# Edge ranges searched partly inside the block loop, with their index on GpSimd and the loop unrolled

## Chip, cores, metric

One core of a Trainium2 chip runs the whole program. The metric is the time of one execution on the device in microseconds (us). Engines: TensorE (PE, its weight loads PEld), VectorE (DVE), ScalarE (ACT), GpSimd (POOL), SyncE (SP, which only issues DMAs here).

## What is computed

A graph layer and a mixture of experts over 6250 nodes of width 256, with 100000 edges of 96 features whose destinations `dst` are sorted:

```python
out1 = segment_sum(edge_attr, dst)            # per node
out2 = where(cnt > 0, segment_max(edge_attr, dst), 0)
out3 = out1 / maximum(cnt, 1)
h = concatenate([ln_x, out1, out2, out3, u[0]], axis=1)
x1 = x + relu(h @ W1 + b1) @ W2 + b2 + ln_x   # ln_x = layernorm(x)
y = layernorm(x1)                             # then top 2 of 16 experts
out = x1 + layernorm(y + moe(y)) * gamma + beta
```

The destinations are `6250 * u**2` of a uniform u, so low nodes have many edges and high nodes few.

## The kernel before

Three stages follow each other.

**Opening.** The 6250 nodes are 50 tiles of 125 (TILES), two to a block (25 blocks, MACROS), and the blocks are worked from the high nodes down. For every node the kernel must know at which edge its range starts. It is found in two steps. ScalarE compares each node with the heads of 625 rows of 160 edges (count_heads, line 815) and picks the row (pick_rows, 830 and 832). GpSimd fetches that row of `dst` for the 125 nodes of a tile by an indirect DMA (line 614), and ScalarE counts in it (count_row, line 824). This goes in ten groups of 5 tiles; SR holds ten fetched rows. GpSimd issues all 50 fetches before it goes on (lines 607 to 615); ScalarE counts all 50 before its first moments (line 878). VectorE turns the counts into start edge, row numbers IX of the two scans, chunk number gatei, and the factors cp, has and rch (index, lines 1420 to 1447): for 20 tiles behind its first chunk of edges, for the other 30 behind its second. SyncE moves each node's start to the node before it (nextn, lines 465 and 466).

**Block loop.** Two chains run side by side. VectorE scans the edges in ten chunks of 128 pieces of 80 edges, also from the end: running sums (line 1381), running maxima (line 1385) and the carry over the pieces (1396 to 1406). SyncE stores sums, maxima and carries to DRAM and then counts up chunk_done (line 470). For each block i GpSimd gathers, by six indirect DMAs (lines 631 to 633), the rows of both scans and the carry at IX. Before that it reads the block's chunk number, copies the block's index columns (line 623), waits for so many chunks and takes one of ten branches. Its order in a block is rows_step: add_rows(i-1) (660), residual(i) (677, 679), cut(i+1) (638), norm1(i+1) (651 to 655), join(i+1) (642 to 646), norm2(i-1) (665 to 670), gather(i+2). The blocks run in pairs inside a hardware loop, hence the copied columns.

ScalarE's order is gnn_step: moments of the next block (878, 883), carry_in(i+1) (861; 865, whose input is the cut; 867; 869), the first four relus of block i (913), moments2 (922, 927), mask_rows(i+1) (893 to 899), the second four relus (913), and the copies of transposed tiles. TensorE does layer 1 in two halves of four banks (1160 to 1164), with the router (1193) between them, the transposes of the next block (1141, 1144), then layer 2 (1174). The second half of layer 1 reuses a bank that the first half's first relu frees.

**Experts.** 113 slots of 128 rows go through their expert's two matrices (1284, 1292), and a last norm follows.

SyncE, ScalarE and GpSimd each run strictly in the order written, so a wait holds up everything behind it on that engine.

## Time and profile before

| | us |
|---|---|
| median of 3 runs | 1287.15 (1284.53 to 1287.29) |
| the profiled execution | 1287.32, its span 1285.6 |
| TensorE busy | 1105.2 (86%) |
| VectorE busy | 803.1 (62%) |
| ScalarE busy | 647.5 (50%) |
| GpSimd busy | 802.0 (62%) |
| mean granted TensorE clock | 0.978 |

A profile comes from one execution. Times in it count from the start of the span. The chain of waits that the page prints gives half of the span to TensorE and a third to VectorE's scans. A wait in it is put down to the event seen last; where a semaphore had long been up, the line names it all the same, so waits are better read from the timeline of the waiting engine.

### The profile page before, as it was taken

To read this page: it belongs to the slowest core of one execution; us is meant where nothing else is said; L and a number is where in the kernel's file an instruction comes from. 1 tells how busy PE (TensorE), PEld (TensorE's weight loads), DVE (VectorE), ACT (ScalarE), POOL (GpSimd) and SP (SyncE) were. 2 spreads that over 40 slices of the span, in tenths; PEclk is the share of its full clock that TensorE was granted. 3 is DMA by queue.
4 is the path that set the end of the run, shared out by engine and by line. 5 is a ranking of instruction groups with operands and counts; after the bars stand their busy time and mean duration, and the time that the engine had idled before them with its cause. 6 is when DMAs were issued, how large, how long until landed. Compare 5 with 4: busy or idle time off the path is not lost.

```text
span 1285.6 us, 27773 instructions
## 1 busy us (share of the span) xinstructions
PE 1105.2 (86%) x6560; PEld 965.7 (75%) x6561; DVE 803.1 (62%) x3060; ACT 647.5 (50%) x1974; POOL 802.0 (62%) x1053
## 2 busy tenths in 40 slices
PE   2002999999999998999999999999999999999914
PEld 1001788888878887887888888889999999989801
DVE  4999999799889989970362401474322222247777
ACT  5863565666566655665665433222232323346544
POOL 4886657766755675666766425555666666656576
PEclk9999999999999998999999999999999999999966
DMA  9995668768767776479111046865666666689744
GB/s 318 279 300 191 238 232 313 254 258 294 257 256 255 285 249 223 173 263 306 46 45 40 28 134 220 303 242 173 203 214 212 204 215 207 217 279 298 249 171 153
DMA packets 131327, 282.71 MB, mean 220 GB/s; under 512 B 25900, under 2 KB 38576, under 8 KB 131114
## 3 DMA queue, kind: packets, MB, share of 16 engines
q1 hardware_dynamic: 94230, 218.41, 49.3%
q0 software_dynamic: 26048, 43.47, 11.1%
q10 hardware_dynamic: 10964, 19.96, 4.5%
q14 instruction: 63, 0.52, 0.1%
q8 instruction: 22, 0.36, 0.1%
HBM read 167.27 MB, written 114.25 MB: 219 GB/s over the span
## 4 chain that ended last, share of the span: by engine, by line
PE 50%; DVE 34%; DMA 6%; issue 5%; POOL 2%; ACT 2%; SPq 1%; POOLq 0%; DVEq 0%; ACTq 0%
PE ps L1284 14%; PE ps L1292 14%; DVE mem L1381 13%; DVE mem L1385 13%; PE ps L1174 5%; PE ps L1160 5%; PE ps L1162 5%; PE ps L1270 2%; DMA mem<-x_normed,mem 2%; DVE mem L1401 2%; PE ps L1210 1%; DMA mem<-piece_carry,mem 1%; DVE mem L1406 1%; DVE mem L1396 1%; DMA mem<-in_edge_attr_dram 1%
## 5 line engine op out<-in xcount | busy, mean ns | idle before, releaser
L1013 ACT ACTIVATE mem<-ps,mem 128x128 f32<-128x128 f32 x452 | 129.3, 368 | 285.1 <-PE ps L1284 283.2
L1284 PEld LDWEIGHTS ps<-mem 128*128 128x128 f32 x1808 | 217.8, 192 | 11.8 <-issue 5.9
L1284 PE MATMUL ps<-mem 128*128 128x128 f32 x1808 | 221.2, 276 | 4.1 <-issue 3.8
L1160 PE MATMUL ps<-mem 128*128 128x250 f32 x800 | 208.4, 383 | 16.4 <-ACT mem L913 14.9
L1292 PE MATMUL ps<-mem 128*128 x904 | 215.2, 381 | 3.7 <-issue 3.2
L1381 DVE TENSOR_TENSOR_SCAN mem<-ps,mem 128x80 f32<-128x80 f32 x960 | 208.0, 304 | 0.3
L1385 DVE TENSOR_TENSOR_SCAN mem<-ps,mem 128x80 f32<-128x80 f32 x960 | 207.8, 313 | 0.0
L1162 PE MATMUL ps<-mem 128*128 128x250 f32 x800 | 204.1, 378 | 0.0
L1174 PE MATMUL ps<-mem 128*125 128x256 f32 x800 | 181.0, 379 | 0.7 <-ACT mem L913 0.7
L1292 PEld LDWEIGHTS ps<-mem 128*128 128x128 f32 x904 | 162.9, 190 | 24.6 <-issue 6.9
L1160 PEld LDWEIGHTS ps<-mem 128*128 128x128 f32 x800 | 152.7, 194 | 35.8 <-ACT mem L913 16.8
L1162 PEld LDWEIGHTS ps<-mem 128*128 128x128 f32 x800 | 153.6, 192 | 18.6
L1174 PEld LDWEIGHTS ps<-mem 128*125 128x125 f32 x800 | 146.3, 188 | 21.1 <-ACT mem L913 1.1
L724 POOL DMA_INDIRECT expert_rows<-mem x90 | 90.9, 1010 | 99.1 <-DVE mem L1659 87.6
L1659 DVE TENSOR_TENSOR mem<-ps,mem 128x256 f32<-128x256 f32 x113 | 48.0, 425 | 148.6 <-PE ps L1292 145.0
L1652 DVE COPY mem<-ps 128x256 f32<-128x256 f32 x113 | 47.8, 423 | 145.9 <-PE ps L1270 142.2
L718 POOL DMA_INDIRECT mem<-x_normed,mem x94 | 93.9, 999 | 30.2 <-issue 15.0
L913 ACT ACTIVATE mem<-ps,mem 128x250 f32<-128x250 f32 x200 | 77.1, 468 | 48.9 <-PE ps L1164 48.9
L1141 PE MATMUL ps<-mem 125*128 125x125 f32 x100 | 20.6, 288 | 91.2 <-ACT mem L899 91.2
L631 POOL DMA_INDIRECT mem<-run_max,mem x50 | 63.7, 1275 | 46.4 <-issue 43.2
L1141 PEld LDWEIGHTS ps<-mem 125*128 125x128 f32 x100 | 11.6, 144 | 98.3 <-issue 98.3
L614 POOL DMA_INDIRECT mem<-in_dst_dram,mem x50 | 62.1, 1242 | 29.5 <-ACT mem L832 14.6
(279 smaller groups left out, 1672.7 us busy)
## 6 DMA issues: line engine op xcount, KB each, us to landing
mem<-in_L_ffn_w_dram SPq DMA_DIRECT2D x129, 512.0 KB, 9.6
run_sum<-mem SPq DMA_DIRECT2D x80, 480.0 KB, 5.6
run_max<-mem SPq DMA_DIRECT2D x80, 480.0 KB, 5.5
mem<-in_edge_attr_dram SPq DMA_DIRECT2D x72, 480.0 KB, 8.1
mem<-expert_rows SPq DMA_DIRECT2D x26, 256.0 KB, 5.0
x_rows<-mem ACTq DMA_DIRECT2D x25, 256.0 KB, 3.0
x_normed<-mem ACTq DMA_DIRECT2D x25, 256.0 KB, 4.0
mem<-in_x_dram ACTq DMA_DIRECT2D x24, 256.0 KB, 4.8
```

Source lines behind the costliest of these rows:

```text
L631: pool.indirect_dma_start(out=GM[b][:, a, :], out_offset=None, in_=s_max[0:edges], in_offset=last).then_inc(gathered[b], 16)
L718: pool.indirect_dma_start(out=XG[b], out_offset=None, in_=x2_d[0:rows], in_offset=bass.IndirectOffsetOnAxis(slot_now[b], 0)).then_inc(xg_g ...
L724: pool.indirect_dma_start(out=ya_d, out_offset=bass.IndirectOffsetOnAxis(into_now[b], 0), in_=YO[b], in_offset=None).then_inc(yo_stored[b] ...
L913: act.activation(H[:, hc, :], bank(H_BANKS[q][hc - q * QUAD], 0, M), ACT.Relu, bias=cbias[:, hc:hc + 1]).then_inc(h_ready, 1)
L1013: ins = act.activation(hT[b][:, c, :], bank(2 + b, c * P, (c + 1) * P), ACT.Relu, bias=eb1c[:, bass.ds(e, 1), c])
L1160: pe.matmul(h, W1x[:, c, hc * P:(hc + 1) * P], XT[b][:, c, :], start=(c == 0), stop=False)
L1162: pe.matmul(h, W1a[:, s, hc * P:(hc + 1) * P], AT[b][:, s, :], start=False, stop=False)
L1174: ins = pe.matmul(bank(5, a * D, (a + 1) * D, NT), H[:, hc, a * NT:(a + 1) * NT], W2[:, hc, :], start=(hc == 0), stop=(hc == HC - 1))
L1284: ins = pe.matmul(bank(2 + b, f * P, (f + 1) * P), w1now[q][:, c, f * P:(f + 1) * P], XgT[b][:, c, :], start=(c == 0), stop=(c == DC - 1))
L1292: ins = pe.matmul(bank(6 + b, 0, D), hT[b][:, c, :], w(c * D, D), start=(c == 0), stop=(c == FC - 1))
L1381: ins = dve.tensor_tensor_scan(out=Sb[:, ::-1, f], data0=keep[b][:, ::-1], data1=Eb[b][:, ::-1, f], initial=0.0, op0=ALU.mult, op1=ALU.add)
L1385: ins = dve.tensor_tensor_scan(out=Eb[b][:, ::-1, f], data0=bound[b][:, ::-1], data1=Eb[b][:, ::-1, f], initial=-FMAX, op0=ALU.min, op1=AL ...
```

## The change

The tiles are split in three. The 20 first ones (FIRST_TILES) and ten more (LATER_TILES) are fetched and counted ahead of the loop, 30 fetches instead of 50; the 20 last (LAST_TILES) are fetched two per block in blocks 0 to 9, into four buffers of their own (SRL), by seek_late on GpSimd, and counted by ScalarE in the same block, ahead of the second relus (count_late). ScalarE's head counts all stay ahead of the loop; the row counts of the sixth five tiles stand behind head group 7 and ahead of head groups 8 and 9, and behind these come block 0's moments.

The index of the first 20 tiles runs on GpSimd, between its 25th and its 26th fetch, as 32 operations each waited for, with the two moves of start edges as DMAs of GpSimd. A power of -1 takes the place of the reciprocal there. The index of the next ten tiles stays on VectorE, behind its second chunk. That of the last 20 runs on GpSimd in four parts, between residual and cut of blocks 10, 11, 12 and 13.

GpSimd's block loop is written out for 25 blocks. Its gathers read the index columns in place. They wait for a number of chunks fixed per block (SCANNED); a branch on the chunk number falls back to all ten chunks if more than that were needed. For the inputs here the fixed number is as large as the needed one or up to three larger.

```diff
-    LATE = TILES - 4 * ST
+    FIRST_TILES, LATER_TILES = slice(TILES - 4 * ST, TILES), slice(TILES - 6 * ST, TILES - 4 * ST)
+    LAST_TILES = slice(0, TILES - 6 * ST)
+    SOUGHT = LAST_TILES.stop // 2
+    EARLY_GATHERS = 6
...
+    SCANNED = [1 if i < 4 else min(LEVELS, 1 + (24 * (i - 2) + 10) // 52) for i in range(MACROS)]
...
+        minus_one = k.take(4 * ST, parts=NT)
...
+        SRL = a.take(4, ROWE, parts=NT, dt=I32)
+        late_junk = [a.take(ROWE, parts=NT) for _ in range(2)]
...
+        def floors(e, op, out, v, n, shift_by):
+            op(e.tensor_scalar(out, v, 1.0 / n, (shift_by + 0.5) / n - 0.5, ALU.mult, ALU.add))
+            op(e.tensor_scalar(out, out, ROUND, None, ALU.add))
+            op(e.tensor_scalar(out, out, ROUND, None, ALU.subtract))
+        def start_edges(e, op, c):
+            op(e.tensor_scalar(startn[:, c], rowf[:, c], float(ROWE), 0.5 * ROWE, ALU.mult, ALU.add))
+            op(e.tensor_scalar(tA[:, c], rows_seen[:, c], 0.5, None, ALU.mult))
+            op(e.tensor_tensor(startn[:, c], startn[:, c], tA[:, c], ALU.add))
+        def start_rows(e, op, c):
+            op(e.tensor_copy(endn[:, c.start:c.stop:2], startn[:, c.start + 1:c.stop:2]))
+            op(e.tensor_scalar(tA[:, c], startn[:, c], float(E - 1), None, ALU.min))
+            floors(e, op, tB[:, c], tA[:, c], T, 0)
+            floors(e, op, tC[:, c], tB[:, c], P, PAD)
+            op(e.tensor_scalar(gatei[:, c.start // 2:c.stop // 2], tC[0:1, c.start:c.stop:2], -1.0, float(CHUNKS), ALU.mult, ALU.add))
+            op(e.tensor_scalar(tC[:, c], tC[:, c], -2.0 * P * T, None, ALU.mult))
+            op(e.tensor_tensor(tA[:, c], tA[:, c], tC[:, c], ALU.add))
+            op(e.tensor_scalar(IX[:, c, 0], tA[:, c], float(T * (PAD + FULL * P)), None, ALU.add))
+        def next_pieces(e, op, c):
+            op(e.tensor_scalar(tB[:, c], tB[:, c], 1.0, None, ALU.add))
+            op(e.tensor_scalar(cp[:, c], tB[:, c], float(T), None, ALU.mult))
+            op(e.tensor_scalar(tB[:, c], tB[:, c], float(PIECES - 1), None, ALU.min))
+            floors(e, op, tC[:, c], tB[:, c], P, PAD)
+            op(e.tensor_scalar(tC[:, c], tC[:, c], -2.0 * P, None, ALU.mult))
+            op(e.tensor_tensor(tB[:, c], tB[:, c], tC[:, c], ALU.add))
+            op(e.tensor_scalar(IX[:, c, 1], tB[:, c], float(PAD + FULL * P), None, ALU.add))
+        def edge_counts(e, op, c, one_over):
+            op(e.tensor_copy(endn[:, c.start + 1:c.stop:2], nextn[:, c.start:c.stop:2]))
+            op(e.tensor_tensor(cp[:, c], endn[:, c], cp[:, c], ALU.subtract))
+            op(e.tensor_scalar(cp[:, c], cp[:, c], 0.0, 1.0, ALU.max, ALU.min))
+            op(e.tensor_tensor(tA[:, c], endn[:, c], startn[:, c], ALU.subtract))
+            op(e.tensor_scalar(has[:, c], tA[:, c], 1.0, None, ALU.min))
+            op(e.tensor_scalar(tA[:, c], tA[:, c], 1.0, None, ALU.max))
+            one_over(tB[:, c], tA[:, c])
+            op(e.tensor_tensor(rch[:, c], tB[:, c], has[:, c], ALU.mult))
...
-                if isinstance(s, int) and s < 2:
-                    lo, hi = ((LATE, TILES), (0, LATE))[s]
-                    sp.wait_ge(starts_ready, s + 1)
-                    sp.dma_start(nextn[0:NT - 1, lo:hi], startn[1:NT, lo:hi]).then_inc(ends_got, 16)
-                    sp.dma_start(nextn[NT - 1:NT, lo:hi], startn[0:1, lo + 2:hi + 2]).then_inc(ends_got, 16)
+                if isinstance(s, int) and s == 1:
+                    c = LATER_TILES
+                    sp.wait_ge(starts_ready, 1)
+                    sp.dma_start(nextn[0:NT - 1, c], startn[1:NT, c]).then_inc(ends_got, 16)
+                    sp.dma_start(nextn[NT - 1:NT, c], startn[0:1, c.start + 2:c.stop + 2]).then_inc(ends_got, 16)
...
-            for n in range(GROUPS):
+            def seek(n):
...
-            pool.wait_ge(index_ready, 1)
-            def gather(i, g, b):
-                level = pool.value_load(gatei[0:1, bass.ds(MACROS - 1 - i, 1)], min_val=1, max_val=LEVELS)
-                hold(pool, turned, i + 1)
-                pool.tensor_copy(IXn[b], IX[:, bass.ds(2 * (MACROS - 1 - i), 2), :]).then_inc(ix_copied, 1)
-                pool.wait_ge(ix_copied, i + 1)
-                hold(pool, chunk_done, level * LEVEL)
-                for lv in range(1, LEVELS + 1):
-                    edges, pieces = lv * LEVEL * P * T, lv * LEVEL * P
-                    with pool.If(level == lv):
-                        for a in range(2):
-                            last, before = (bass.IndirectOffsetOnAxis(IXn[b][:, a, n:n + 1], 0) for n in range(2))
-                            pool.indirect_dma_start(out=GM[b][:, a, :], out_offset=None, in_=s_max[0:edges], in_offset=last).then_inc(gathered[b], 16)
-                            pool.indirect_dma_start(out=GS[b][:, a, :], out_offset=None, in_=s_sum[0:edges], in_offset=last).then_inc(gathered[b], 16)
-                            pool.indirect_dma_start(out=GC[b][:, a, :], out_offset=None, in_=carry[0:pieces], in_offset=before).then_inc(gathered[b], 16)
+            def seek_late(j):
+                if j == 0:
+                    pool.wait_ge(rows_ready, GROUPS)
+                if j >= 4:
+                    pool.wait_ge(late_counted, j - 3)
+                pool.indirect_dma_start(out=SRL[:, j % 4, :], out_offset=None, in_=dst2,
+                                        in_offset=bass.IndirectOffsetOnAxis(rowU[:, j:j + 1], 0)).then_inc(late_got[j % 4], 16)
+            ix = Steps(pool, index_step)
+            def op(ins):
+                ix.mark(ins)
+                ix.wait()
+            def pool_over(out, v):
+                op(pool.tensor_tensor(out, v, minus_one[:, 0:v.shape[1]], ALU.pow))
+            def end_edges(c):
+                pool.dma_start(nextn[0:NT - 1, c], startn[1:NT, c]).then_inc(pool_ends, 16)
+                pool.dma_start(nextn[NT - 1:NT, c], startn[0:1, c.start + 2:c.stop + 2]).then_inc(pool_ends, 16)
+            for n in range(5):
+                seek(n)
+            pool.wait_ge(row_counted, TILES - FIRST_TILES.start)
+            start_edges(pool, op, FIRST_TILES)
+            end_edges(FIRST_TILES)
+            start_rows(pool, op, FIRST_TILES)
+            next_pieces(pool, op, FIRST_TILES)
+            pool.wait_ge(pool_ends, 32)
+            edge_counts(pool, op, FIRST_TILES, pool_over)
+            pool.sem_inc(index_ready, 1)
+            seek(5)
+            def gather_rows(i, levels):
+                b, m = i % 2, MACROS - 1 - i
+                edges, pieces = levels * LEVEL * P * T, levels * LEVEL * P
+                pool.wait_ge(chunk_done, levels * LEVEL)
+                for a in range(2):
+                    last, before = (bass.IndirectOffsetOnAxis(IX[:, 2 * m + a, n:n + 1], 0) for n in range(2))
+                    pool.indirect_dma_start(out=GM[b][:, a, :], out_offset=None, in_=s_max[0:edges], in_offset=last).then_inc(gathered[b], 16)
+                    pool.indirect_dma_start(out=GS[b][:, a, :], out_offset=None, in_=s_sum[0:edges], in_offset=last).then_inc(gathered[b], 16)
+                    pool.indirect_dma_start(out=GC[b][:, a, :], out_offset=None, in_=carry[0:pieces], in_offset=before).then_inc(gathered[b], 16)
+            def gather(i):
+                m, near = MACROS - 1 - i, SCANNED[i]
+                if near == LEVELS:
+                    gather_rows(i, LEVELS)
+                else:
+                    level = pool.value_load(gatei[0:1, m:m + 1], min_val=1, max_val=LEVELS)
+                    with pool.If(level < near + 1):
+                        gather_rows(i, near)
+                    with pool.If(level > near):
+                        gather_rows(i, LEVELS)
...
-            def rows_step(i, g, b):
+            def rows_step(i):
+                g, b = i // 2, i % 2
                 more = not isinstance(i, int) or i + 1 < MACROS
                 norm = not isinstance(i, int) or i >= 1
                 if norm:
                     add_rows(i - 1)
                 residual(i, g, b)
+                if i < SOUGHT:
+                    seek_late(2 * i)
+                elif i == SOUGHT:
+                    pool.wait_ge(late_counted, 2 * SOUGHT)
+                    start_edges(pool, op, LAST_TILES)
+                    end_edges(LAST_TILES)
+                elif i == SOUGHT + 1:
+                    start_rows(pool, op, LAST_TILES)
+                elif i == SOUGHT + 2:
+                    next_pieces(pool, op, LAST_TILES)
+                elif i == SOUGHT + 3:
+                    pool.wait_ge(pool_ends, 64)
+                    edge_counts(pool, op, LAST_TILES, pool_over)
                 if more:
                     cut(*after(i, g, b))
                     norm1(i + 1)
                     join(*after(i, g, b))
+                if i < SOUGHT:
+                    seek_late(2 * i + 1)
                 if norm:
                     norm2(i - 1)
-                if not isinstance(i, int) or i + 2 < MACROS:
-                    gather(*after(i, g, b, 2))
+                if i + 2 < MACROS:
+                    if i + 2 == (TILES - FIRST_TILES.start) // 2:
+                        pool.wait_ge(index_ready, 2)
+                    gather(i + 2)
             pool.sem_inc(joined, 1)
-            gather(0, 0, 0)
+            gather(0)
             norm1(0)
             cut(0, 0, 0)
             join(0, 0, 0)
-            gather(1, 0, 1)
-            rows_step(0, 0, 0)
-            rows_step(1, 0, 1)
-            pool.wait_ge(index_ready, 2)
-            in_pairs(pool, MACROS, rows_step, ahead=3, first=2)
+            gather(1)
+            for i in range(MACROS):
+                rows_step(i)
...
+                if n - 2 < EARLY_GATHERS:
+                    count_row(n - 2)
+            def count_late(i, g, b):
+                for a in range(2):
+                    j = bass.ds(2 * i + a, 1)
+                    act.wait_ge(late_got[2 * b + a], (g + 1) * 16)
+                    if not isinstance(i, int) or i >= 1:
+                        act.wait_ge(late_counted, 2 * i + a - 1)
+                    act.activation(late_junk[a], SRL[:, 2 * b + a, :], ACT.Sign, bias=below[:, j], scale=-1.0,
+                                   accum_out=rows_seen[:, j]).then_inc(late_counted, 1)
...
+                if late:
+                    count_late(i, g, b)
...
+            gnn_step(0, 0, 0, late=True)
+            gnn_step(1, 0, 1, late=True)
+            in_pairs(act, SOUGHT, lambda i, g, b: gnn_step(i, g, b, EARLY_M - i, True), first=2)
+            in_pairs(act, EARLY_M, lambda i, g, b: gnn_step(i, g, b, EARLY_M - i), first=SOUGHT)
...
-            dve.wait_ge(row_counted, TILES - LATE)
-            op(dve.memset(startn[:, TILES:TILES + 2], float(E)))
-            index(LATE, TILES, 1)
             edges(1, 0, 1)
-            dve.wait_ge(row_counted, TILES)
-            index(0, LATE, 2)
+            dve.wait_ge(row_counted, TILES - LATER_TILES.start)
+            start_edges(dve, op, LATER_TILES)
+            dve.sem_inc(starts_ready, 1)
+            start_rows(dve, op, LATER_TILES)
+            next_pieces(dve, op, LATER_TILES)
+            dve.wait_ge(ends_got, 32)
+            edge_counts(dve, op, LATER_TILES, lambda out, v: op(dve.reciprocal(out, v)))
+            dve.sem_inc(index_ready, 1)
```

## Rows read from the trace of the kernel before

**Rows 1.** Windows: busy of PE, PEld, DVE, ACT, POOL; clock, DMA share, GB/s.

```profile
0.00:119.70 119.70, 9.29 (x27) 6.29 (x28) 100.09 (x437) 75.64 (x248) 78.90 (x89) 1.00 0.87 278
119.70:776.70 657.00, 638.84 (x3497) 546.15 (x3497) 482.03 (x2023) 383.65 (x1141) 406.47 (x510) 0.99 0.59 207
```

**Rows 2.** Timeline: start, length, engine, line, operation, [idle before <-releaser], us.

```profile
57.41 1.21 POOL L614 DMA_INDIRECT mem<-in_dst_dram,mem  x1 [0.30 <-issue]
...
97.48 1.22 POOL L631 DMA_INDIRECT mem<-run_max,mem  x1 [1.04 <-issue]
...
106.63 0.73 POOL L653 TENSOR_TENSOR mem<-mem 125x2 f32<-125x2 f32 x1
...
111.93 0.59 POOL L638 TENSOR_TENSOR mem<-mem 125x192 f32<-125x192 f32 x1 [4.29 <-DMA mem<-piece_carry,mem]
```

**Rows 3.** Timeline of ScalarE at the start.

```profile
71.65 0.76 ACT L815 ACTIVATE mem<-ps,mem 125x625 f32<-125x625 f32 x1
...
99.04 0.40 ACT L878 ACTIVATE mem<-mem 125x256 f32<-125x256 f32 x1
...
101.16 0.19 ACT L883 ACTIVATION_READ_ACCUMULATOR mem<-mem 125x1 f32 x1
```

**Rows 4.** Timeline of SyncE's queue: loads behind the first chunk.

```profile
78.36 4.02 SPq L434 DMA_DIRECT2D mem<-in_edge_attr_dram  x8
```

**Rows 5.** Landings from issue: L614; L631, then L633, over 95:200.

```profile
DMA to landing us min/median/max: 3.3/6.9/8.7
DMA to landing us min/median/max: 3.1/4.8/7.2
DMA to landing us min/median/max: 3.6/6.8/7.8
```

**Rows 6.** GpSimd's groups by line (count, busy us, mean ns); VectorE's timeline, index.

```profile
L653 POOL TENSOR_TENSOR mem<-mem 125x2 f32<-125x2 f32 x25 | 18.4, 735 | 2.1
...
L604 POOL TENSOR_SCALAR mem<-mem 125x50 f32<-125x50 f32 x1 | 0.4, 369 | 0.0
...
75.22 0.18 DVE L1417 TENSOR_SCALAR mem<-mem 125x20 f32<-125x20 f32 x1
```

**Rows 7.** Timeline of block 5: TensorE, ScalarE, GpSimd.

```profile
258.25 1.11 PE L1160 MATMUL ps<-mem 128*128 128x250 f32 x4
...
256.33 0.62 ACT L865 ACTIVATE mem<-mem 125x96 f32<-125x96 f32 x2
...
257.75 1.53 ACT L913 ACTIVATE mem<-ps,mem 128x250 f32<-128x250 f32 x4
...
266.05 1.55 ACT L913 ACTIVATE mem<-ps,mem 128x250 f32<-128x250 f32 x4 [0.79 <-PE ps L1164]
...
255.14 0.59 POOL L638 TENSOR_TENSOR mem<-mem 125x192 f32<-125x192 f32 x1
...
261.77 0.19 POOL L665 TENSOR_SCALAR mem<-mem 125x2 f32<-125x2 f32 x1 [1.47 <-ACT mem L927]
```

**Rows 8.** Waits (us, times, longest); TensorE's timeline; one window's clock.

```profile
PE ps L1160 <- ACT mem L913: 14.9, 13, 3.4
...
359.08 1.20 PE L1160 MATMUL ps<-mem 128*128 128x250 f32 x2 [2.00 <-ACT mem L913]
...
487.29 2.04 PE L1160 MATMUL ps<-mem 128*128 128x250 f32 x4 [3.39 <-ACT mem L913]
...
591.53 2.03 PE L1160 MATMUL ps<-mem 128*128 128x250 f32 x4 [2.79 <-ACT mem L913]
...
487.00:493.00 6.00, 5.71 (x16) 4.73 (x17) 6.00 (x30) 4.96 (x18) 3.33 (x7) 0.58 0.46 169
```

**Rows 9.** Timeline of GpSimd: first gather of block 6.

```profile
242.23 1.33 POOL L631 DMA_INDIRECT mem<-run_max,mem  x1 [1.38 <-issue]
```

**Rows 10.** Timeline of SyncE's queue: loads behind the third chunk.

```profile
200.44 4.18 SPq L434 DMA_DIRECT2D mem<-in_edge_attr_dram  x8
```

**Rows 11.** Timeline of VectorE: a turn of the scan loop begins.

```profile
249.70 0.25 DVE L1373 TENSOR_TENSOR ps<-mem 128x79 f32 x1 [5.76 <-issue]
```

48 lines of the change are left out of this document (7 added, 41 removed).

## Prediction

> **What bounds the kernel now.** I read the windows first. Up to 119.7 us TensorE does almost nothing (9.3 us busy), from 119.7 to 776.7 it is busy for 638.8 of 657 us [rows 1]. So the opening costs its full length, and in the block loop anything that makes TensorE wait costs its full length too. The expert stage behind it holds no step of the change and starts from what the loop delivers; I let it shift with the loop's end.
>
> Then the timeline of GpSimd at the start. The 26th of its 50 row gathers starts at 57.41 and each takes 1.21 us with 0.30 before it; block 0's own gathers start only at 97.48, behind all 50, and its cut runs at 111.93 [rows 2]. ScalarE ends block 0's moments at 101.35 (99.04 to 101.16 and 0.19), so it has about 10 us to spare there [rows 3]. The first chunk is known to be in DRAM at 78.36, when SyncE goes past its wait and loads the next edges [rows 4]. This is the room of the change: 78.4 against 97.5.
>
> Then one block of the loop, block 5, on three engines [rows 7]. TensorE begins its second half at 258.25 without a gap, and the relu that frees its bank started at 257.75. That relu stands in ScalarE's order behind the carries, whose sign step (line 865, 256.33) waits for GpSimd's cut (255.14 to 255.73). So the cut has 0.6 us of slack and the relu nearly none. Last the waits: TensorE stood at this place 13 times, 14.9 us in all; the large ones are 2.00, 3.39 and 2.79 us in blocks 9, 14 and 18, behind late carry gathers (block 0 has another of 2.5) [rows 8]. Of the other nine, 4.2 us together, the timeline puts 2.2 in blocks 1 to 9, 0.6 in blocks 10 to 13 and 1.4 behind.
>
> **Start: gathers.** GpSimd does 25 row gathers, done at 57.1. The 20 first counts are there by then. Now 32 small operations run on GpSimd, each waiting for itself: 3, then two DMAs, then 12, 9 and 8. The nearest rows are 0.73 us for the two-column power with 0.27 from the operation before it to its start [rows 2], and 0.37 for a plain operation with 50 columns [rows 6]; I take 0.29 a piece. The DMAs are not shown on GpSimd; between 0.35 and 1.5 us each, and I take 1.35, nearest to its own indirect ones. So 57.1 + 0.9 + 2.7 + 21 x 0.29 = 66.8, then 7 x 0.29 = 2.0 and the power with 20 columns. With two columns it takes 0.73, some 0.54 more than a plain operation [rows 6]. If that excess is per column, 20 take 5.6 us; if it is fixed, 0.7. I take 5.6, as the work is done element by element, and keep 0.7. Index ready at 75 (70). Five more row gathers: 83 (78). Gathers of block 0 start at about 84 (79), instead of 97.5.
>
> The Trainium skill, GPSIMD Engine Reference, section Performance versus the Vector engine, says that ordinary elementwise work is about twice as slow on GpSimd, with two software hops per instruction. Here 0.29 a piece stands against 0.21 from start to start on VectorE's index (0.18 long [rows 6]), less than the rule says. By the rule the 31 plain operations would take 13 us instead of 9, and the sum would be 4 us higher, 1295.
>
> **Start: ScalarE takes over.** It counts rows 25 to 29 only behind head group 7, and head groups 8 and 9 stand behind them. The last of these gathers starts at 81.4 (76.6) and lands 6.9 later [rows 5]; then come two head groups, each five counts of 0.76 and about 0.6 for picking the rows, 4.4, and 2.3 us of moments [rows 3]. That gives 99.9 (95.1) instead of 101.16. GpSimd's norm waits for them, and the cut stands behind it, 1.3 later: 101 (96) instead of 111.9. The gathered rows, starting 8 us after the first and landing 6.8 after that [rows 5], come at 98.5 and are no longer last. Gain 11 (16). VectorE's scan is about 8 us earlier because its first index is gone.
>
> **Blocks 1 to 9.** Two row gathers a block. The second stands in a gap of 1.47 us [rows 7] and is free. The first stands between residual and cut: 1.5 us less 0.6 of slack is 0.9, and I take 0.8, as the rows gathered for the next block leave GpSimd a little sooner. ScalarE's relu and with it TensorE's second half begin that much later, 1.8 in block 1, where TensorE waits already: 8 x 0.8 + 1.8 = 8. ScalarE's two counts of 0.41 stand ahead of the second relu, where it idles 0.79 [rows 7], if the second row has landed. It starts 3 us behind the first relu and must land in 5.2; the loop's first gathers took 3.1 to 7.2 [rows 5], over it by 0.4 on average: 3 in all. Against this, the gathers of a block leave earlier: the index copy, the hold and the chain of ten branches, 1.38 before line 631 in block 6 [rows 9] on top of what stands before line 623, shrink by 1.4 to 2.3 us, more in late blocks. The 2.00 and the 2.2 go, with 1.6 of low clock behind the first. Net: 11 less 5.8, 5 lost. Block 0 gains 0.6.
>
> **Blocks 10 to 13.** The index of the last 20 tiles stands between residual and cut: 3.6 us (3 operations, two DMAs), 3.5 (12), 2.6 (9), and 2.0 plus the power. Less 0.75 each that the block hides: 2.8, 2.7, 1.9 and 6.9 (2.0 with a fixed price), sum 14.3 (9.4). TensorE at rest also loses its clock: after the stop of 3.39 us the granted clock was 0.58 over 487 to 493, about half (1.2 GHz) for most of it [rows 8]; the stops of 2.8 and 2.0 cost 1.9 and 1.6 more in the same way, the one of 2.5 in block 0 nothing. I add 1.5 per block, 6. Less the old 0.6: 20 lost (15).
>
> **Blocks 14 to 24.** No added work, gathers 2 us earlier. Of 3.39 + 2.79 + 1.4 some 2 remain, and the low clock behind them (2.3 + 1.9) goes: 10 gained.
>
> **The new fixed chunk numbers.** Gathers now wait for a number of chunks fixed per block, up to three more than the block needs. Nearest is block 6 with chunk 3: its gathers start at 242.23, chunk 3 was there at 200.44 [rows 9, 10]. 42 us of distance, shrunk by 8 at most: nothing.
>
> **Sum**, in the profiled execution (1287.32 us, span 1285.6, practically the median 1287.15): -11 - 0.6 + 5 + 20 - 10 = +3.5, that is 1291 us. This case spans 1286 to 1298, with the clock price (0 to 8) and the DMAs on GpSimd (0.35 to 1.5 each).
>
> **Rivals.**
> 1. The power hardly grows with the columns. Start 16, blocks 10 to 13 15: -16 - 0.6 + 5 + 15 - 10 = -6.6, 1280.5. For it: the other GpSimd operations grow little (0.37 for 50 columns). Against: this one alone is 3.7 times as long at two. It decides at 3.9 us for 20 columns, where the sum is zero (each us of the power counts twice). Chance 0.26. This is the case on the other side.
> 2. The added work in the loop is hidden: the gap before line 660 and the earlier gathers take it up, and the cut isn't what the relu waits for. Then blocks 1 to 9 win 4 and blocks 10 to 13 cost 8: -11 - 0.6 - 4 + 8 - 10 = -17.6, 1270. Against: 0.6 us of slack is read directly. Chance 0.13.
> 3. ScalarE's loop becomes too long. In VectorE's loop there is a stop of 5.76 us without a releaser at every second turn [rows 11], which I read as code coming in. If ScalarE's body, longer by the counts, did this in its 4 turns of blocks 2 to 9, with 3 us of idle to take it up, that adds 4 x 2.8 = 11: 1302. ScalarE's rows show no such stop now. Chance 0.08. The Trainium skill, Runtime: NRT & Kernel Launch, section Instruction fetch mechanics, says that a taken branch to outside two pages of 256 instructions forces a fetch; by it this happens only if the body outgrows them, and GpSimd's unrolled order never pays it.
> 4. The row gathers land late throughout, as in the opening (6.9) instead of as in the loop: 9 x 1.7 instead of 3, 12 more: 1303. Chance 0.1.
> 5. The fixed chunk numbers do stop GpSimd after all: a block waits for a chunk, 10 us or more: 1300. Chance 0.03.
>
> **Chances.** Forecast 0.40; the rivals 0.26, 0.13, 0.08, 0.10, 0.03. The range from 1273 to 1302 leaves out part of rivals 2 and 4. A measurement can tell some 0.2% from no change, 2.6 us. Faster by more: rivals 1 and 2 but for their edge, 0.38. Within: 0.17, the lower end of the forecast and the upper end of rival 1. Slower by more: 0.45. Cases of both signs hold most of the chance, so the forecast's own range is 1286 to 1298.
>
> **What would show it.** Block 0's cut at 101 us, ScalarE idle before its count of row 25, index on GpSimd from 57 to 75 with one power near 5.6 us; about 0.8 us of wait at line 1160's second half in each of blocks 2 to 9, four waits of 2 to 7 us in blocks 10 to 13, fewer and shorter ones behind. Wrong, if the power takes under 2 us, if the cut in the blocks with row gathers ends before the sign step asks for it, or if the stage behind 776 us changes its own length.

## The result and the profile after

The changed kernel takes 1296.0 us (median of 6, 1293.3 to 1300.0) where the kernel before takes 1286.1 (median of 6, 1284.5 to 1288.7) on the same chip: ratio 1.0062, 95% interval 1.0033 to 1.0092. It is slower, by 0.6%, clear of noise. Its profiled execution took 1293.27 us, with a span of 1291.0; the span before was 1285.6, so the two traces differ by 5.4 us.

The windows of the changed kernel, to be read beside [rows 1] (busy of PE, PEld, DVE, ACT, POOL; granted clock, DMA share, GB/s):

```profile
0.00:108.00 108.00, 8.55 (x27) 5.99 (x28) 89.92 (x389) 64.96 (x204) 66.86 (x101) 0.57 0.89 293
108.00:770.00 662.00, 633.00 (x3439) 540.42 (x3440) 479.33 (x2044) 390.28 (x1176) 436.98 (x538) 0.98 0.59 204
770.00:1291.00 521.00, 468.50 (x3096) 421.50 (x3094) 221.91 (x603) 192.17 (x595) 319.68 (x460) 0.95 0.68 223
```

Before the loop TensorE has almost nothing to do up to 109.9 us instead of 119.8, and yet the span is longer, so what stands behind the opening must have lost more than the opening won. (The mean granted clock is 0.931 where the trace of before has 0.978. That difference lies in the opening, 0.57 against 1.00, where TensorE is busy for 9 us only; from the first transposes to the 25th block's it is 0.98 and 0.99.) To see where the time went, I took the start of every block's transposes (line 1255, line 1141 before) from TensorE's timeline and call the start of block n's "turn n". The stretch from turn 1 to turn 10 is then TensorE's work of blocks 1 to 9. Five of the turns, of the changed kernel:

```profile
109.92 0.65 PE L1255 MATMUL ps<-mem 125*128 125x125 f32 x2 [82.16 <-ACT mem L1010]
...
131.37 0.43 PE L1255 MATMUL ps<-mem 125*128 125x125 f32 x2
...
365.14 0.43 PE L1255 MATMUL ps<-mem 125*128 125x125 f32 x2
...
483.65 0.43 PE L1255 MATMUL ps<-mem 125*128 125x125 f32 x2
...
745.77 0.38 PE L1255 MATMUL ps<-mem 125*128 125x125 f32 x2
```

They are turns 0, 1, 10, 14 and 24. A table by these marks carries most of what follows, so the experiments' rows stand in it too (us):

| kernel | turn 0 at | 0 to 1 | 1 to 10 | 10 to 14 | 14 to 24 | behind 24 | span |
|---|---|---|---|---|---|---|---|
| before | 119.8 | 23.1 | 225.4 | 98.6 | 273.7 | 545.0 | 1285.6 |
| after | 109.9 | 21.5 | 233.8 | 118.5 | 262.1 | 545.2 | 1291.0 |
| before, second trace | 118.9 | 22.5 | 230.2 | 103.5 | 266.4 | 550.0 | 1291.5 |
| after, second trace | 111.0 | 22.7 | 231.3 | 120.3 | 262.1 | 548.8 | 1296.3 |
| e_unroll | 117.5 | 21.6 | 219.1 | 98.5 | 262.1 | 545.1 | 1264.0 |
| e_index_moved | 111.2 | 22.4 | 231.8 | 107.2 | 262.1 | 546.6 | 1281.2 |
| e_seek_moved | 109.6 | 21.5 | 245.1 | 120.9 | 262.1 | 544.7 | 1303.9 |
| e_moved_both | 109.8 | 21.5 | 245.2 | 111.7 | 265.6 | 545.5 | 1299.2 |
| e_late_all | 110.8 | 21.3 | 226.8 | 105.8 | 267.5 | 550.5 | 1282.6 |
| e_count_behind | 110.2 | 21.6 | 226.0 | 107.4 | 262.9 | 550.3 | 1278.3 |
| e_power_one | 106.3 | 21.6 | 233.0 | 116.6 | 262.3 | 557.9 | 1297.7 |
| e_open | 101.0 | 22.4 | 238.6 | 119.6 | 262.1 | 551.6 | 1295.3 |
| e_best | 101.3 | 21.2 | 227.6 | 107.9 | 265.6 | 555.7 | 1279.4 |
| e_best_spread | 101.9 | 21.1 | 223.7 | 99.1 | 263.1 | 548.6 | 1257.6 |

Before to after, first traces: -9.9, -1.6, +8.4, +19.9, -11.6, +0.2, sum 5.4. The second traces give -7.9, +0.2, +1.1, +16.8, -4.3, -1.2, sum 4.8 before rounding. So the sum repeats, but a stretch of the loop differs by up to 7 us between two traces of the kernel before (by up to 2.5 between those of the changed kernel), and each other kernel has one trace: differences of 2 or 3 us in one column are not told from this scatter. The stage behind turn 24 is the same code in all of them and took 545 to 558 us; it was longer in the later comparisons, for the kernel before as well (550.0 in its second trace). So kernels of different comparisons are compared here up to turn 24, and whole times by their ratio to the kernel before on the same chip.

TensorE's waits in the loop of the changed kernel, to be read beside [rows 8] (us in total, times, longest us):

```profile
PE ps L1274 <- ACT mem L1024: 19.7, 15, 5.1
PE ps L1288 <- ACT mem L1024: 6.6, 5, 3.2
```

Line 1274 is the second half of layer 1 (1160 before), 14.9 us in 13 times there; line 1288 is layer 2, which waits for the second relus (1174 before, 0.7 us once).

The opening on GpSimd, beside [rows 2]: the 25th row gather, the index's first operation, the power, the 26th row gather, block 0's first gather and the cut.

```profile
55.08 1.21 POOL L665 DMA_INDIRECT mem<-in_dst_dram,mem  x1 [0.30 <-issue]
56.37 0.21 POOL L440 TENSOR_SCALAR mem<-mem 125x20 f32<-125x20 f32 x1
...
69.76 3.74 POOL L683 TENSOR_TENSOR mem<-mem 125x20 f32<-125x20 f32 x1
73.58 0.23 POOL L471 TENSOR_TENSOR mem<-mem 125x20 f32<-125x20 f32 x1
74.88 1.38 POOL L665 DMA_INDIRECT mem<-in_dst_dram,mem  x1 [1.07 <-issue]
...
82.63 1.21 POOL L707 DMA_INDIRECT mem<-run_max,mem  x1 [0.30 <-issue]
...
102.09 0.59 POOL L725 TENSOR_TENSOR mem<-mem 125x192 f32<-125x192 f32 x1
```

### The profile page after: what moved, and what is told of

Same layout as the page of the kernel before. It is cut to its first block, busy times and chain, and to the rows that moved or that the text cites. A ratio compares the mean times of both kernels' runs of the same rounds, so it can differ in the third digit from the quotient of the medians.

```text
span 1291.0 us, 27234 instructions
## 1 busy us (share of the span) xinstructions
PE 1110.0 (86%) x6560; PEld 967.9 (75%) x6561; DVE 791.2 (61%) x3035; ACT 647.4 (50%) x1974; POOL 823.5 (64%) x1097
## 4 chain that ended last, share of the span: by engine, by line
PE 55%; POOL 22%; issue 12%; ACT 5%; DVE 3%; DMA 2%; POOLq 1%; ACTq 0%; SPq 0%; DVEq 0%
PE ps L1398 16%; PE ps L1406 15%; PE ps L1288 6%; PE ps L1274 6%; PE ps L1276 6%; POOL mem L707 3%; POOL mem L708 3%; POOL mem L709 3%; PE ps L1384 2%; POOL mem L665 2%; POOL mem L764 1%; POOL mem L747 1%; PE ps L1324 1%; DMA mem<-in_dst_dram,mem 1%; POOL mem L673 1%
## 5 line engine op out<-in xcount | busy, mean ns | idle before, releaser
L1274 PE MATMUL ps<-mem 128*128 128x250 f32 x800 | 209.3, 385 | 21.2 <-ACT mem L1024 19.7
L1274 PEld LDWEIGHTS ps<-mem 128*128 128x128 f32 x800 | 153.4, 194 | 41.0 <-ACT mem L1024 21.8
L747 POOL TENSOR_TENSOR mem<-mem 125x512 f32<-125x512 f32 x25 | 32.5, 1299 | 93.6 <-ACT mem L1074 93.6
L1255 PEld LDWEIGHTS ps<-mem 125*128 125x128 f32 x100 | 11.6, 144 | 89.3 <-issue 89.3
```

Source lines behind the costliest of these rows:

```text
L1274: pe.matmul(h, W1x[:, c, hc * P:(hc + 1) * P], XT[b][:, c, :], start=(c == 0), stop=False)
```

## Experiments

**1. The unrolled loop alone (e_unroll).** The kernel before with one part of the change:

```diff
-            rows_step(0, 0, 0)
-            rows_step(1, 0, 1)
-            pool.wait_ge(index_ready, 2)
-            in_pairs(pool, MACROS, rows_step, ahead=3, first=2)
+            for i in range(MACROS):
+                if i == 2:
+                    pool.wait_ge(index_ready, 2)
+                rows_step(i, i // 2, i % 2)
```

and gather as in the changed kernel (gather_rows, SCANNED, no IXn).

> The kernel before, with one part of the change alone: GpSimd's block loop unrolled, the gathers' index columns read from fixed places (no copy of the index, no wait for the block's turn ahead of it) and the chunk numbers fixed. Row searches and index stay as before. Theory (the forecast's step on blocks 14 to 24): the gathers leave about 2 us earlier in each block and TensorE's waits for ScalarE's turned copies go; about 24.4 us per block where before shows 24.5 to 29, so -10 us in blocks 14 to 24 and -3 to -8 in blocks 1 to 13: time about 1272 (1268 to 1277), opening and expert stage unchanged. Rival: the shorter late blocks of the changed kernel come from something else (where its dips of the clock happen to fall): then this kernel stands within 3 us of the kernel before.

Measured: 1266.1 us, ratio 0.984 (0.981 to 0.987), below the range expected. The theory holds, and by more than it asked for. Turns 14 to 24 take 262.1 us, exactly what they take in the changed kernel, and turns 1 to 10 take 219.1, the 24.4 a block at which TensorE is not kept waiting. The whole loop's waits of the kind of [rows 8]:

```profile
PE ps L1166 <- ACT mem L919: 2.1, 4, 0.7
```

So this one part is worth 21.6 us of span (1285.6 to 1264.0; by the ratios 1.6%). It is itself three things, the unrolled order, the index read in place and the fixed chunk numbers, and no run tells them apart. The changed kernel contains it and is 5.4 us slower than before: its other parts together cost 27 us. Where they do so can be read against this row of the table: the early opening gives 7.6 (117.5 to 109.9), the row searches in the loop cost 14.7 (219.1 to 233.8; 12.2 by the second trace), the index in the loop 20.0 (98.5 to 118.5; 21.8), and the other stretches agree within 0.1 us.

**2. The index behind the gathers (e_index_moved).** The four parts at the end of rows_step, behind gather(i + 2); the power behind the gather for block 15:

```diff
-                elif i == SOUGHT:
-                    pool.wait_ge(late_counted, 2 * SOUGHT)
-                    start_edges(pool, op, LAST_TILES)
...
                     gather(i + 2)
+                if i == SOUGHT:
+                    pool.wait_ge(late_counted, 2 * SOUGHT)
+                    start_edges(pool, op, LAST_TILES)
...
```

> The changed kernel with the last 20 tiles' index moved from between residual sum and cut of blocks 10 to 13 to the end of GpSimd's steps 10 to 13, behind the join and behind the gathers for the block after next. Theory (forecast's step on blocks 10 to 13): the stalls of TensorE's turns 11 to 14 (2.1, 3.1, 2.2, 5.1 us and the low clock behind them) come from the place alone; GpSimd idles some 3.7 us per block behind the join, so they go nearly whole: turns 10 to 14 in about 99 us instead of 119, time 17 us below the changed kernel. Rival: the index work is too much for GpSimd wherever it stands (the power alone 3.7 us): half of the 20 us stays, time 8 to 10 us below the changed kernel, and the sum of the rows shows up as waits at add_rows and cut of the next block.

Measured: 1284.5 us, ratio 0.997 (0.9955 to 0.9986), 0.9% below the changed kernel's ratio, some 12 us: between the two. Turns 10 to 14 take 107.2. Of the 20 us the place explains 11.3; 8.7 stay. Experiment 5 takes them away by cutting the work into smaller pieces.

**3. The first row gather behind the join (e_seek_moved), and both moves (e_moved_both).**

```diff
-                if i < SOUGHT:
-                    seek_late(2 * i)
...
                 if i < SOUGHT:
+                    seek_late(2 * i)
                     seek_late(2 * i + 1)
```

> The changed kernel with the even row gather of blocks 0 to 9 moved from between residual sum and cut to behind the join, beside the odd one. Theory (forecast's step on blocks 1 to 9): each of these gathers delays the cut by 1.2 us and TensorE's turn by 0.6 us; these 0.6 us waits go, turns 1 to 10 take 3 to 6 us less than the 252 of the changed kernel, time 4 us below it. Rival: what lengthens these blocks is ScalarE's count in front of the second relus, which waits for rows that land late: then the even row lands later still, the waits at the second layer's last tiles (1.5, 0.5, 3.2, 0.7 us now) grow, and the time is the same or 3 to 6 us above the changed kernel.

> The changed kernel with both moves: both row gathers of blocks 0 to 9 behind the join, and the last 20 tiles' index at the end of GpSimd's steps 10 to 13. Theory: the two gains add, about 21 us below the changed kernel, some 1275. Rival (rows that land late keep ScalarE's count in front of the second relus): only the index part is gained, some 1279 to 1285.

Measured: 1310.1 us, ratio 1.0187 (1.0146 to 1.0228), and 1301.2 us, ratio 1.0123 (1.0091 to 1.0154). The theory falls. The rivals hold and were sized too low: e_seek_moved's said 6 us above the changed kernel at most, and it is 14 above it; e_moved_both's said 1285 at most. Turns 1 to 10 take 245 us, 11 more than in the changed kernel. e_seek_moved's waits in the loop:

```profile
PE ps L1273 <- ACT mem L1023: 16.4, 9, 5.1
PE ps L1287 <- ACT mem L1023: 14.5, 7, 3.0
```

The waits of 0.6 us at the second half of layer 1 are gone, as expected (9 waits instead of 15), but layer 2 now waits 14.5 us instead of 6.6. ScalarE's timeline in the changed kernel shows the mechanism already, at block 7, with TensorE's layer 2 behind it:

```profile
313.19 0.43 ACT L965 ACTIVATE mem<-mem 125x160 f32<-125x160 int32 x1 [3.73 <-DMA mem<-in_dst_dram,mem]
313.53 0.19 ACT L965 ACTIVATION_READ_ACCUMULATOR mem<-mem  x1
313.62 1.53 ACT L1024 ACTIVATE mem<-ps,mem 128x250 f32<-128x250 f32 x4
```

```profile
314.12 5.41 PE L1288 MATMUL ps<-mem 128*125 128x256 f32 x16 [3.23 <-ACT mem L1024]
```

ScalarE stands 3.73 us at the count (line 965) for a row that has not landed; the second relus are behind it in its order, and TensorE waits for them. Of the 18 row gathers from 119 to 350 us the landing took

```profile
DMA to landing us min/median/max: 3.2/5.0/8.8
```

**4. The counts a block later (e_late_all, e_count_behind).** ScalarE counts in block i + 1 what GpSimd fetched in block i:

```diff
                 if late:
-                    count_late(i, g, b)
+                    count_late(i - 1, g if b else g - 1, 1 - b)
```

e_late_all is e_moved_both with this; e_count_behind is e_index_moved with this, so that the first row gather stays between residual and cut.

> The changed kernel with both row gathers of blocks 0 to 9 behind the join and the last 20 tiles' index at the end of GpSimd's steps, as in e_moved_both, and with one thing more: ScalarE counts the rows fetched in block i in block i+1, not in block i. The same row gathers and the same counts stand on both engines. Theory now (after e_seek_moved was 14 us slower than the changed kernel, with eight waits of the second layer's last tiles for ScalarE, up to 3.0 us each): what lengthens blocks 1 to 9 is ScalarE standing at the count for a row that has not landed, with the second relus behind it. A block later every row has landed: these waits are gone, blocks 1 to 10 take 24.4 to 24.8 us each, time some 1272 (1268 to 1277), 28 us below e_moved_both. Rival: GpSimd's own cycle is what is full (two gathers of rows, 3 us, where it has some 2 to 3.7 us to spare per block): then blocks 1 to 9 stay at 26 to 28 us and the time is 1285 or more.

> The changed kernel with the last tiles' index at the end of GpSimd's steps and ScalarE's counts a block later, but with each block's even row gather left where the change puts it, between residual sum and cut. It tells the place of the gather from the count. Theory: the waits of the second layer's last tiles for ScalarE (1.5, 0.5, 3.2, 0.7 us) go, and the waits of 0.6 us at the second half of the first layer, one per block, stay, because the gather still delays the cut. Turns 1 to 10 take 225 to 228 us (233.7 in the changed kernel, 226.8 with the gathers behind the join, 219.2 with no row gathers in the loop); time 2 to 4 us below that of e_index_moved against the kernel before, ratio 0.994 to 0.996. Rival: with the counts gone the even gather is hidden in its place too, turns 1 to 10 in 220 to 222, ratio 0.990.

Measured: 1284.4 us, ratio 0.9934 (0.9902 to 0.9967), and 1284.9 us, ratio 0.9932 (0.9902 to 0.9961). Turns 1 to 10 fall from 245.2 to 226.8 with the gathers behind the join, and from 231.8 to 226.0 with the first one in its place; layer 2 no longer waits for ScalarE in blocks 1 to 9 of either. So the landing was a large part of what made the searches dear, 5.8 us in the changed order (e_index_moved has the changed kernel's code in these blocks; its trace and the two of the changed kernel have 231.3 to 233.8). e_count_behind's turns 1 to 10 were expected in 225 to 228 and came in 226.0. e_late_all was expected at 1268 to 1277 and missed: the waits of layer 2 went, yet some 7 us above e_unroll's 219.1 remain in blocks 1 to 9, whichever of the two places the gather has. e_count_behind shows them as waits of 0.49 to 0.61 us at the second half of layer 1, one in each of blocks 2 to 9, and one of 1.47 in block 1. In e_late_all GpSimd is seen to be out of time, block 4 to 5:

```profile
228.93 1.22 POOL L679 DMA_INDIRECT mem<-in_dst_dram,mem  x1 [0.30 <-issue]
230.23 0.19 POOL L758 TENSOR_SCALAR mem<-mem 125x2 f32<-125x2 f32 x1
...
241.87 1.21 POOL L715 DMA_INDIRECT mem<-piece_carry,mem  x1 [0.30 <-issue]
243.11 1.28 POOL L753 TENSOR_TENSOR mem<-mem 125x512 f32<-125x512 f32 x1
```

add_rows (L753) starts right behind the last gather, with no idle time; in e_unroll the same step, at 245.71, waited 1.90 us for ScalarE:

```profile
245.71 1.26 POOL L666 TENSOR_TENSOR mem<-mem 125x512 f32<-125x512 f32 x1 [1.90 <-ACT mem L969]
...
256.40 0.19 POOL L671 TENSOR_SCALAR mem<-mem 125x2 f32<-125x2 f32 x1 [1.60 <-ACT mem L933]
```

These are the two largest waits of GpSimd for another engine in a block of 24.4 us, in blocks 2 to 9 1.4 to 1.6 us ahead of norm2 and 0.6 to 2.1, mostly about 2, ahead of add_rows. (It also stands for 1.2 to 2.7 us ahead of each block's first gather, with no releaser shown; no run put work there.) Two row gathers with their 0.30 ahead are 3.0.

**5. Work cut to the gaps (e_best, e_best_spread), with the opening of e_open.** e_best puts together the moves, the later counts and e_open's opening (below). e_best_spread also cuts GpSimd's extra work to the two gaps: one row gather in each, the index in seven pieces, the power in two halves of 10 columns:

```diff
+            def behind_join(i):
...
+                if i == SOUGHT + 1:
+                    start_rows(pool, op, c, 0)
+                elif i == SOUGHT + 2:
+                    next_pieces(pool, op, c, 0)
+                elif i == SOUGHT + 3:
+                    edge_lengths(pool, op, c, 1)
...
+            def behind_gathers(i):
...
+                elif i == SOUGHT + 3:
+                    edge_shares(pool, op, slice(10, 20), pool_over)
+                elif i == SOUGHT + 4:
+                    edge_shares(pool, op, slice(0, 10), pool_over)
...
                 if i < SOUGHT:
-                    seek_late(2 * i + 1)
+                    seek_late(2 * i)
+                else:
+                    behind_join(i)
...
+                if i < SOUGHT:
+                    seek_late(2 * i + 1)
+                else:
+                    behind_gathers(i)
```

> All of it together: the row gathers and the last tiles' index behind the join, the counts a block later, and the reordered opening. If the parts add: e_late_all less 5 to 7 us, some 1266 (1260 to 1272), which is about what the unrolled loop alone gave on the kernel before (1266.1). If GpSimd's cycle is full, it stays above that by the row gathers' 3 us in each of nine blocks, 1280 or more.

> e_best with GpSimd's extra work cut to the two gaps that the unrolled loop shows in each block: about 1.5 us behind the join (ahead of norm2) and 1.6 to 2.1 us behind the gathers (ahead of add_rows). One row gather stands in each gap instead of both behind the join, the index of the last 20 tiles is spread over seven pieces of 1 to 2 us, and its power is taken in two halves of 10 columns in blocks 13 and 14. Theory (an idle gap of its own size hides each piece; what is over it stretches the block): blocks 2 to 20 at 24.4 us as with the unrolled loop alone, the opening as in e_open, so first turn at 101, the 25th turn at 703 to 708 instead of 719 (unrolled loop alone) and 724 (e_best); ratio about 0.972 (0.967 to 0.977). Rival: the landing of the row gathers' packets or the pool of DMA queues is what costs, or the clock dips behind any stall: 25th turn at 715 or later, ratio 0.981 or more.

Measured: 1279.0 us, ratio 0.9882 (0.9834 to 0.9931), and 1261.5 us, ratio 0.9752 (0.9708 to 0.9795). The time of e_best doesn't decide between its two cases: 1279.0 is near the second, while its ratio, taken on the first chip's 1286.1, would be 1271, at the slow end of the first. Its trace speaks for the second: turns 1 to 10 take 227.6, 8.5 above e_unroll. e_best_spread is the fastest kernel here, 2.5% below the kernel before. Turns 10 to 14 take 99.1 us instead of 107.9 and turns 14 to 24 263.1 instead of 265.6: with the pieces in the gaps the index costs 0.6 us there and 1.0 behind, measured against e_unroll, instead of the 20.0 of the changed kernel. Turns 1 to 10 take 223.7, 4.6 above e_unroll. A block of e_best_spread on GpSimd:

```profile
304.89 1.21 POOL L685 DMA_INDIRECT mem<-in_dst_dram,mem  x1 [0.30 <-issue]
307.14 1.28 POOL L758 TENSOR_TENSOR mem<-mem 125x512 f32<-125x512 f32 x1 [1.04 <-ACT mem L1105]
...
316.55 1.33 POOL L685 DMA_INDIRECT mem<-in_dst_dram,mem  x1 [0.19 <-issue]
317.95 0.19 POOL L763 TENSOR_SCALAR mem<-mem 125x2 f32<-125x2 f32 x1
```

The gather ahead of add_rows leaves 1.04 us of idle time, the one ahead of norm2 just fills its gap. Turn 24 was expected at 703 to 708 and came at 709.0 (e_unroll 718.9, e_best 723.7). What the last 4.6 us are was not taken apart. One part may be a fixed chunk number: at 194.83 GpSimd's first gather of a block stands behind a wait of 1.35 us for SyncE's line 531, which counts up chunk_done.

**6. The opening (e_power_one, e_open).** e_power_one takes the power over one column in place of 20:

```diff
-                op(pool.tensor_tensor(out, v, minus_one[:, 0:v.shape[1]], ALU.pow))
+                op(pool.tensor_tensor(out[:, 0:1], v[:, 0:1], minus_one[:, 0:1], ALU.pow))
```

> The changed kernel with the power that makes 1/count in the index on GpSimd taken over one column instead of 20, in both places (19 of 20 columns of the reciprocal counts are left out, so the mean over edges is not the reference's). The profile shows 3.74 us for the 20 columns. Theory: in the opening GpSimd's index delays the gathers of rows 25 to 29, for which ScalarE waits 8.3 us in all at its counts, so the opening is 3.5 us shorter (first turn at 106.4 instead of 109.9), and the stall of block 13's index goes down from 5.1 to some 1.5 us; in all 6 to 8 us below the changed kernel. Rival: the opening is bounded by ScalarE's own head counts and by the landings: first turn stays within 1 us of 109.9, in all 3 to 4 us.

Measured: 1297.9 us, ratio 1.0057 (1.0031 to 1.0082), no different from the changed kernel's 1.0062. In the trace the theory's parts are there: turn 0 at 106.3 instead of 109.9, the wait behind block 13's index 2.09 us instead of 5.07, turn 24 6.0 us earlier. The stage behind it took 557.9 us, the longest of all, against 550 in the kernel before's second trace. That it lost what the loop had won is what the row shows; why it was longer I did not find. (The expectation counted four of ScalarE's waits for rows 25 to 29, 8.3 us; with the 11.39 us ahead of row 25 they are 19.7.)

e_open reorders GpSimd's opening:

```diff
-            for n in range(5):
+            for n in range(EARLY_GATHERS):
                 seek(n)
...
-            edge_counts(pool, op, FIRST_TILES, pool_over)
+            edge_lengths(pool, op, FIRST_TILES)
             pool.sem_inc(index_ready, 1)
-            seek(5)
...
             gather(0)
+            edge_shares(pool, op, FIRST_TILES, pool_over)
             norm1(0)
```

> The changed kernel with its opening reordered on GpSimd: the gathers of rows 25 to 29 ahead of the index of the first 20 tiles instead of behind it, and the power and its product behind block 0's gathers; VectorE's index of the next ten tiles waits for GpSimd's. Theory: ScalarE's 8.3 us of waits for rows 25 to 29 go and the power is hidden behind the landing of block 0's gathers, which then start 3.7 us earlier; ScalarE's head counts and moments end about 92, the carries start when block 0's gathers have landed, at 94 to 96 instead of 100.7; first turn at 103 to 105, and the time 5 to 7 us below the changed kernel. Rival: five more row gathers ahead of the index fill the DMA queues and the index waits for nothing less, so that block 0's gathers land no earlier: within 1 us.

Measured: 1296.0 us, ratio 1.0004 (0.9968 to 1.0041). By the ratios that is 7 us below the changed kernel, but the two intervals overlap, so the times alone don't show a gain. The trace shows it at the start: turn 0 comes at 101.0, better than expected. Of ScalarE's waits for rows 25 to 29 (19.7 us in the changed kernel) one of 2.2 us is left, what it waits for is block 0's gathers, and the power lies beside their landing:

```profile
87.81 3.60 POOL L689 TENSOR_TENSOR mem<-mem 125x20 f32<-125x20 f32 x1
...
93.22 0.60 POOL L730 TENSOR_TENSOR mem<-mem 125x192 f32<-125x192 f32 x1
```

```profile
93.26 0.64 ACT L978 ACTIVATE mem<-mem 125x96 f32<-125x96 f32 x2 [10.79 <-DMA mem<-piece_carry,mem]
```

About half of the 8.9 us was lost again in blocks 1 to 9 (238.6 instead of 233.8), where layer 2 waited 6.9 us for ScalarE (5.2 in the changed kernel). In e_best and e_best_spread, whose counts come a block later, the early turn 0 is kept.

**7. Second traces.**

> The changed kernel once more, for a second trace: in the first comparison its profiled execution was the fastest of its six (1293.3 to 1300.0), 5.4 us above the kernel before by the spans, where the medians differ by 9.9. Theory: its parts that don't depend on landings repeat within 1 us (first turn at 110, turns 10 to 14 in 118 to 119, turns 14 to 24 in 262), and what varies is the stretch in which ScalarE counts rows in front of the second relus, by how late they land: turns 0 to 10 in 255 to 262. Rival: the expert stage, whose code is the same in both kernels, varies as much (510 us in both first traces) and has nothing to do with the change.

> The kernel before once more on the same chip, for a second trace. Theory: turns 0 to 10 in 248 to 250, 10 to 14 in 98 to 101, 14 to 24 in 272 to 276, and the expert stage as long as in the changed kernel's second trace, so that what is left of the difference lies in the block loop. Rival: the expert stage differs between the two traces by 5 us or more.

Measured: the changed kernel, 1301.4 us median, ratio 1.0062 (1.002 to 1.0104) on that chip. Both spans are longer, by 5.3 and 5.9 us, of which 3.6 and 5.0 lie behind turn 24; their difference is 4.8 again. In both traces of the changed kernel turns 14 to 24 take 262.1 and four waits of 2.1, 3.1, 2.2 and 5.1 us stand in blocks 10 to 13. Its turns 10 to 14 came in 120.3, above the 118 to 119 expected, and its turns 0 to 10 in 254.0, just below the 255 to 262. What varies more is the kernel before: turns 1 to 10 took 225.4 and 230.2, turns 10 to 14 98.6 and 103.5, turns 14 to 24 273.7 and 266.4, so all three of its expected stretches were missed. Its waits fall in other blocks from trace to trace. The stage behind turn 24 differs by 1.2 us between the two second traces, so the rival on it falls.

## Why the prediction was right, step by step

The forecast was 1291 us and slower. By its own sum it holds: +3.5 forecast, +5.4 in the spans, 4.8 in the second pair of traces. The medians differ by more, 9.9, and the median of 1296.0 is close to the upper end of the case's range of 1286 to 1298. That range does not follow from the two terms named for it: a clock price of 0 to 8 in place of 6 and four DMAs of 0.35 to 1.5 in place of 1.35 give 1281 to 1294. So the sign and the parts below are what the forecast got right; that the median fell into the range is partly luck. The first profiled execution was the fastest of the changed kernel's six; in which blocks the others lose their time isn't traced. None of the three signs of being wrong came: the power took 3.74 us, the sign step waited for the cut, and the stage behind the loop took 545.0 and 545.2 us.

**Opening: forecast -11, measured -9.9 (second traces -7.9).** The power was priced at 5.6 us and took 3.74, and the DMAs on GpSimd at 1.35 and took 0.65 and 0.56. But three operations that were priced at 0.29 took 1.33, 0.76 and 0.72, so the index ended at 73.8 instead of 75 and block 0's gathers started at 82.6 instead of 84. The cut still came at 102.1 instead of 101: the last row gather started at 81.1 and had landed at 89.1, 8.0 later where 6.9 was taken. That ScalarE is what the cut waits for, through GpSimd's norm (9.42 us of idle time ahead of line 738), is as forecast, and so is its idle time ahead of the count of row 25, 11.39 us. The plain operations took 0.29 to 0.35 from start to start, VectorE's 0.21, 1.4 to 1.7 times as long. The Trainium skill (GPSIMD Engine Reference, Performance versus the Vector engine) says about twice, and gives 1.96 for an addition with N=2048; for these operations on 20 columns it is too much. The forecast's figure by that rule, 4 us more, counts the index in the opening only; the same operations stand a second time in blocks 10 to 13.

**Block 0: forecast -0.6, measured -1.6 (second traces +0.2).** That is within the scatter of the traces.

**Blocks 1 to 9: forecast +5, measured +8.4 (second traces +1.1).** The two pairs lie on either side of the forecast, because the kernel before took 225.4 and 230.2. The terms show more than the sum. The mis-sized one is the late second row. The recovered part was 5.8 forecast and 6.3 measured (225.4 to 219.1 in e_unroll). The first gather's delay was put at 8. In the changed kernel the sign step waited for the cut in each of blocks 2 to 9, mostly for 0.8 to 0.9 us as forecast, and TensorE for 0.5 to 0.6 of it. With the counts a block later, where only this wait is left, blocks 1 to 9 take 6.9 more than in e_unroll (226.0 less 219.1), 5.4 of it waits. The counts for rows not yet landed were put at 3 and cost the rest of 14.7: 7.8. The windows split it: 5.2 are three waits of layer 2, and TensorE was busy for 222.3 us in place of 219.9. (The second trace gives 5.3 instead of 7.8.) The forecast took the landing's excess over 5.2 us as 0.4 on average; an average hides that one landing of up to 8.8 stops ScalarE for 3.7 and TensorE for 3.2. Rival 4 came near this, but its condition does not hold: the rows were not late throughout (median 5.0, not 6.9), only some were, and its price of 15 was too high.

**Blocks 10 to 13: forecast +20, measured +19.9 (second traces +16.8).** The stalls were forecast at 2.8, 2.7, 1.9 and 6.9, and were 2.13, 3.08, 2.18 and 5.07, 12.5 instead of 14.3; the last one is smaller by the power's price. The low clock was priced at 6; the windows of the four blocks show it (columns as in [rows 1]):

```profile
365.14:392.83 27.69, 24.86 (x138) 21.00 (x134) 27.69 (x130) 16.22 (x49) 18.36 (x26) 1.00 0.52 188
392.83:422.83 30.00, 26.92 (x138) 22.64 (x135) 28.04 (x121) 15.79 (x47) 21.20 (x35) 0.89 0.84 308
422.83:451.06 28.23, 26.05 (x139) 22.05 (x135) 27.48 (x120) 15.80 (x47) 17.00 (x28) 0.94 0.68 251
451.06:483.65 32.59, 27.52 (x139) 23.09 (x135) 27.20 (x126) 15.80 (x47) 23.61 (x30) 0.90 0.73 240
```

TensorE's busy time in them is 105.3 us, for the same work that takes 98.0 in e_unroll, and the granted clock is 0.89 to 0.94 in three. That is 7.3. So the near agreement of 19.9 with 20 is partly luck: the stalls were 1.8 less than forecast and the longer busy time 1.3 more. Rival 2 (the added work is hidden) is refuted here and, by the waits for the cut, in blocks 1 to 9.

**Blocks 14 to 24: forecast -10, measured -11.6 in the first traces, -4.3 in the second.** The mechanism was right, its size is not settled by the pairs: e_unroll shows the same 262.1 us with none of the change's other parts. The forecast took three large waits of the trace of before as a fixture of blocks 9, 14 and 18; the second trace has them elsewhere, and smaller. The unrolled loop takes them away wherever they fall.

**Fixed chunk numbers: 0 forecast.** GpSimd's idle time ahead of line 707, the first gather for each tile, names no transfer and no chunk, and the longest such gap is 2.4 us:

```profile
L707 POOL DMA_INDIRECT mem<-run_max,mem x50: 1206/1240/1612, 82.6 to 710.5; - x50
its engine sat idle before it (us, times) until:
  issue: 39.7, 50
```

Rival 5 falls for this kernel. Two of the reordered kernels do show one such wait each, e_late_all 1.7 us and e_best_spread 1.4, and the kernel before itself had two, 3.2 us in all, ahead of line 631.

**Power: rival 1.** It was to decide at 3.9 us. It took 3.74 us for 20 columns, 2.00 for 10 (e_best_spread) and 0.72 for two, about 0.17 a column: it does grow with the columns, less than taken. By the forecast's own rule the sum would then be zero; it is +5.4, since the shorter power was met by three slow operations and a late row in the opening and by the counts in the loop.

**ScalarE's code: rival 3.** No stop without a releaser shows in its loop; what it waited for at line 965 were landings, 10.4 us in five waits.

## What to carry to other kernels

Before work is put on an engine in a loop, list that engine's idle gaps of one iteration with their lengths and cut the work to them: here 20 row gathers and an index cost 35 us where the change had put them, and about 6 cut to the gaps with the counts a block later. On an engine that works in written order, don't take up a transfer in the iteration that issued it where it can be taken up one later: the wait then follows the longest landing and not the average, and here the later count took 5.8 us off nine blocks. Time each part of a compound change alone: here one part was worth 1.6% and the others hid it. And take two traces of both kernels before a stretch of a few us is read as an effect.
